# A two-layer graph network: one subtile in every two groups of tiles fetched row by row by SyncE

## The chip, the cores and the metric

The kernel runs on one core of a Trainium2 chip, in one launch. The metric is the device time of one execution in microseconds, the median of several runs. A core has TensorE (PE, matrix products), VectorE (DVE), ScalarE (ACT), GpSimd (POOL) and SyncE (SP); 16 DMA engines move data between device memory and the core's SBUF. Each engine runs its own stream of instructions and waits for the others through semaphores.

## The reference

A graph has 6250 nodes of 128 features and 200,000 edges, sorted by target (`dst`). Two layers run one after the other, each behind a layer norm and a ReLU and each added to `x`:

```
# layer 1: attention, 8 heads of 16
z  = h @ W;  el = z.attn_l;  er = z.attn_r
e  = leaky_relu(el[src] + er[dst], 0.2);  a = exp(e - max over dst)
out[dst] = sum(z[src] * a) / sum(a) + bias

# layer 2: an edge network (MUL = 32)
tpw = silu(silu(edge_attr_8 @ A1 + b1) @ A2 + b2) @ A3          # 4 x 32 weights per edge
messages from s[src], v[src] (s: 32, v: 32 x 3), edge_attr_4 and tpw
out[dst] = (sum of messages / 10) @ W_out
```

What matters here: in each layer, every edge needs one row of a node table, chosen by `src`. That is 200,000 random rows of 576 bytes (`z_tab`) and 200,000 of 512 bytes (`up_tab`).

## The kernel before

The edges are cut into 196 tiles (`NG`) of 1024 edges (`GE`), each of 8 subtiles (`T`) of 128 edges, one edge per partition. Four tiles (`U`) make a group; there are 49 groups (`GI`). The last tile has 3 subtiles (`LT`).

The program goes through these stages:

1. Set-up and the first node pass: norm and the product with `W`, whose rows are stored in `z_tab`.
2. Layer 1 over the groups. For every subtile POOL issues one indirect DMA (`gather`, L436) that brings 128 rows of `z_tab` into `rows[:, s, t, :]`, where `s` is the tile's slot (four slots) and `t` the subtile. DVE adds the target's score (L957, L958, L962), ACT takes the exponential (L555), DVE multiplies the rows by it (L966), and TensorE sums the products by target with a one-hot matrix (L1225), which DVE adds to the sums in SBUF (L883). In the middle of a group DVE finishes the node blocks that are complete by then (`finish_block`, L902 to L923) and SP stores them in `up_tab` (`store_up`, L372).
3. Layer 2 over the same groups, with rows of `up_tab`, two halves of four subtiles per tile (L1067 to L1079 for one half). SP loads the edge features two groups ahead (`load_ef` L390 and `load_y` L386, into two buffers each) and stores finished blocks of the output (L382).

What sets the order: each engine's stream is written out by hand. POOL, for group q and slot s, holds until TensorE has summed slot (s + 1) % 4 of the group before (slot 0 of the same group for s = 3), and then issues the 8 gathers of slot s. Each gather adds 16 to the semaphore `rows0` (subtiles 0 to 3) or `rows1` (4 to 7) of its slot, and DVE waits for `landed` on both. `msg1` of a slot counts the tiles that DVE has multiplied. `hold` is a wait that a register's value may enter, followed by a semaphore increment.

`groups` runs a body over 24 pairs of groups in a loop (`r`), with e = 0 and e = 1 written out in it, and once more for the 49th group. `blocks(eng, kind, at, work)` reads two words of the table `ready`, checks them and does `work` for the blocks between them, one per group on the mean. SP's part of layer 1 is before the change only a loop of 49 `store_up`; in layer 2 it is one `four_tiles` per group, that holds for `h1` (the edge network's first product of the group) ahead of `load_ef` and for `msg1` of slot 3 ahead of `load_y`. POOL waits for all stores of `up_tab` before layer 2.

Of the kernel before, what the change touches and what calls it, by code (L numbers as in the profile page):

```python
# [32 lines left out]
T = 8  # L33
# [8 lines left out]
PARTS = 64 + QUADS  # L42
ERP = 6 * HEADS
# [23 lines left out]
def gnn_kernel(nc, x, src, dst, dst_lin, edge_y, edge_f, bias, front, weights, out):  # L67

    with ExitStack() as ctx:
        def sb(name, shape, dt=F32):  # L70
            return ctx.enter_context(nc.sbuf_tensor(name, shape, dt))
# [66 lines left out]
        dst_rel = sb("dst_rel", [P, NG, T])  # L138
# [22 lines left out]
        rows = sb("rows", [P, U, T, ZW])  # L161
# [9 lines left out]
        def part(at, *shape, parts=P):  # L171
# [5 lines left out]
            if len(shape) == 1:  # L177
# [7 lines left out]
        tab_sb = rows[:, :, :, :].rearrange("p u t f -> p (u t) f")  # L185
# [52 lines left out]
                 ("x0", "x1", "front", "weights", "dst", "lin", "src", "bias", "win")}  # L238
# [6 lines left out]
            "sums_cleared", "ready_set", "cleared")}  # L245

        def named(tag, names):
            return {n: sem(f"{tag}_{n}") for n in names}
# [15 lines left out]
        s_l1 = named("edges", ("open", "er_sum")) | slot_sems("edges", ("spread", "square", "turned", "er", "scored", "score",  # L264
                                                         "exp", "msg0", "msg1", "agg", "added", "rows0", "rows1"))
        s_l2 = named("l2", ("h1", "h2", "tp", "first", "weighted", "dotted")) | slot_sems("l2", ("h1_act", "h2_act")) \
# [9 lines left out]
        def hold(eng, s, value):  # L276

            eng.wait_ge(s, value)
            eng.sem_inc(passed, 1)
# [10 lines left out]
        def last_blocks(eng, work):  # L290

            lo = eng.value_load(ready[0:1, GI + 1:GI + 2], min_val=0, max_val=NB - 1)
            with eng.Fori(lo, NB) as b:
                work(b)

        def groups(eng, body):

            with eng.Fori(0, GI // 2) as r:
                for e in range(2):
# [6 lines left out]
                   "rows1": [GI * 16 * HT] * (U - 1) + [(GI - 1) * 16 * HT]}  # L306
# [18 lines left out]
        def _(sp):  # L325
# [49 lines left out]

            sp.wait_ge(G["ready_set"], 1)
            with sp.Fori(0, NB) as b:
                store_up(b)
# [14 lines left out]
            with sp.Fori(0, passes1) as k:  # L393
                for buf in range(2):
                    load_ef(buf, buf)
                    load_y(buf, buf)

                def four_tiles(q, r, e):
                    n = sp.snap((passes1 + k) * GI + q + 1, min_val=1, max_val=2 * PASSES1 * GI)
                    m = sp.snap(k * (NG + AHEAD) + q * U, min_val=0, max_val=PASSES1 * (NG + AHEAD))  # L400
                    blocks(sp, mybir.EngineType.SP, q, store_block)
                    if isinstance(r, int):
                        return
# [6 lines left out]
                hold(sp, s_l2["h1"], (k + 1) * (NG + AHEAD))  # L410
                hold(sp, s_l1["added"][U - 1], (passes1 + k + 1) * QUADS)
# [14 lines left out]
        def _(pool):  # L426
# [7 lines left out]
            def gather(s, indices, table, width, done, n=T):  # L434
                for t in range(n):
                    pool.indirect_dma_start(out=rows[:, s, t, 0:width], out_offset=None, in_=table,  # L436
                                            in_offset=bass.IndirectOffsetOnAxis(ap=indices[:, t:t + 1], axis=0))\
                        .then_inc(done[t // HT], 16)
# [7 lines left out]
            with pool.If(general > 0):  # L446
                with pool.Fori(0, NG) as g:
                    hold(pool, s_max["idx"], g + 1)
                    gather(0, idx_max, z_tab, ZW, (s_max["rows"],) * 2)
# [164 lines left out]
        def _(dve):  # L614
# [234 lines left out]
            set_columns()  # L849
            own.after(v.tensor_copy(iota_l1, iota[:, :]))  # L850
# [76 lines left out]
            with dve.Fori(0, passes1) as k:  # L927
# [6 lines left out]
                def four_tiles(q, last):  # L934
# [3 lines left out]
                    landed = dve.snap(q * (16 * HT) + 16 * HT, min_val=16 * HT, max_val=GI * 16 * HT)  # L938
                    _, slots = nc.values_load_multi_w_load_instructions(
# [3 lines left out]
                    for s in range(U):  # L943
                        h = s % 2
                        ts = slice(0, LT if last and s == U - 1 else T)
                        el_e = rows[:, s, ts, MW:ZW]

                        if last and s == U - 1:
                            dve.wait_ge(s_l1["rows0"][s], ROWS_IN["rows0"][s])
                        else:  # L950
                            dve.wait_ge(s_l1["rows0"][s], landed)
                            dve.wait_ge(s_l1["rows1"][s], landed)
                        if s == 0:
                            dve.wait_ge(s_l1["added"][2], n)
                        else:
# [13 lines left out]
                            in1=rows[:, s, ts, 0:MW].rearrange("p t (h f) -> p t h f", f=RW),  # L969
# [59 lines left out]
            with dve.Fori(0, passes1) as k:  # L1029
# [8 lines left out]
                def four_tiles(q, r, e):  # L1038
# [4 lines left out]
                    landed = dve.snap(q * (16 * HT) + 16 * HT, min_val=16 * HT, max_val=GI * 16 * HT)  # L1043
                    _, low = nc.values_load_multi_w_load_instructions(
# [6 lines left out]
                    for s in range(U):  # L1051
                        h = s % 2
                        short = isinstance(r, int) and s == U - 1
                        for hf in range(1 if short else 2):
                            half = "rows0" if hf == 0 else "rows1"
                            dve.wait_ge(s_l1[half][s], ROWS_IN[half][s] if short else landed)
                            ts = slice(hf * HT, hf * HT + HT)
                            count = halves + (2 * s + hf + 1)
                            vecs = rows[:, s, ts, 0:96].rearrange("p t (i u) -> p t i u", u=MUL)
                            scal = rows[:, s, ts, 96:128]  # L1060
# [337 lines left out]
```

## Time and profile before

| | us |
|---|---|
| median of 3 runs | 4030.65 (4030.31 to 4036.2) |
| the profiled execution | 4040.77 |
| its span, first to last instruction | 4038.6 |
| mean granted TensorE clock | 0.806 of full speed |

The profile is of one execution. "Busy" is the time that an engine's instructions take; register work, branches and the issuing of DMAs are not counted in it. Layer 1 lies between about 95 and 2041 us of the span, layer 2 between about 2063 and 4028. The granted clock is 6 tenths in nearly all of layer 1 and 9 tenths in layer 2. In both, the slices of the page read 7 tenths busy for POOL, and the DMA engines are about 22% busy and move some 60 GB/s. A name with q behind it (SPq, DVEq, PEldq) is that engine's sequencer, which does register work and issues DMAs.

### The profile page before, as it was taken

The page shows a single profiled execution, that of the slowest core. Times are in us where ns is not written, and L with a number is a line of the kernel's source. Part 1 is how long each engine was busy: PE and PEld are TensorE (multiplying, and loading weights), DVE is VectorE, ACT ScalarE, POOL GpSimd, SP SyncE. Part 2 cuts the span into 40 slices and gives each one's busy share as a digit, 9 for nine tenths or more (in the row PEclk, how much of TensorE's full clock was granted, in tenths as well). Part 3 has the DMA queues.
Part 4 walks back from the last instruction along what each step waited for, and adds up shares of the span by engine and source line. Part 5 has one row for each costly group of instructions (what it writes and reads, how often), then busy time and mean ns, then how long its engine had stood idle before and what let it go on. Part 6 is the DMA issues. An engine that isn't in the chain of part 4 may idle for free.

```text
span 4038.6 us, 45135 instructions
## 1 busy us (share of the span) xinstructions
PE 2624.4 (65%) x11198; PEld 1908.9 (47%) x11199; DVE 2492.2 (62%) x6079; ACT 1012.0 (25%) x1447; POOL 2967.5 (73%) x3136
## 2 busy tenths in 40 slices
PE   3544454545555545445568888787888888888787
PEld 2444444444444444444445555555555555555554
DVE  7444444444444444444367777777877777777777
ACT  4333333333333333333231111111111111111111
POOL 2777777777777777777757777777777777777775
PEclk8666666666666666666679999999999999999999
DMA  4222222222222222222212222221222222222221
GB/s 126 61 60 61 60 61 60 60 60 60 60 60 60 60 60 61 60 60 61 60 49 59 59 59 60 58 60 57 60 58 59 59 59 59 59 60 59 59 59 48
DMA packets 139546, 245.74 MB, mean 61 GB/s; under 512 B 53965, under 2 KB 85815, under 8 KB 139415
## 3 DMA queue, kind: packets, MB, share of 16 engines
q0 software_dynamic: 100032, 217.87, 19.6%
q1 hardware_dynamic: 39352, 26.89, 2.3%
q10 hardware_dynamic: 144, 0.80, 0.1%
q14 instruction: 13, 0.10, 0.0%
q8 instruction: 5, 0.08, 0.0%
HBM read 235.32 MB, written 10.03 MB: 61 GB/s over the span
## 4 chain that ended last, share of the span: by engine, by line
POOL 54%; issue 23%; PE 9%; DVE 7%; DMA 4%; DVEq 1%; POOLq 0%; ACT 0%; ACTq 0%; SPq 0%
POOL rows L436 54%; PE pair L1225 5%; DMA rows<-z_tab,idx 3%; PE pair L1299 2%; DVE share L966 2%; DMA rows<-up_tab,idx 1%; DVE acc L869 1%; PE pair L1256 1%; PE pair L1139 0%; DVE share L957 0%; PE pair L1246 0%; DVE share L1074 0%; PE pair L1270 0%; PE pair L1250 0%; DVE share L1070 0%
## 5 line engine op out<-in xcount | busy, mean ns | idle before, releaser
L436 POOL DMA_INDIRECT rows<-z_tab,idx x1563 | 1488.3, 952 | 546.7 <-issue 525.3
L436 POOL DMA_INDIRECT rows<-up_tab,idx x1563 | 1477.7, 945 | 502.4 <-issue 486.6
L1225 PE MATMUL pair<-share,acc 128*128 128x136 f32 x3126 | 754.8, 433 | 842.2 <-DVE share L966 842.2
L1225 PEld LDWEIGHTS pair<-share,acc 128*128 128x128 f32 x3126 | 700.5, 326 | 975.9 <-DVE share L966 974.3
L1299 PE MATMUL pair<-share,acc 128*128 128x256 f32 x3126 | 808.7, 403 | 297.5 <-DVE share L1079 295.9
L1299 PEld LDWEIGHTS pair<-share,acc 128*128 128x128 f32 x3126 | 580.0, 195 | 677.8 <-DVE share L1079 576.3
L957 DVE TENSOR_TENSOR share<-rows,share 128x64 f32<-128x64 f32 x196 | 44.3, 226 | 899.9 <-DMA rows<-z_tab,idx 899.1
L1067 DVE TENSOR_TENSOR share<-rows,pair 128x384 f32<-128x384 f32 x391 | 216.6, 554 | 330.9 <-DMA rows<-up_tab,idx 320.4
L1256 PE MATMUL pair<-weights_sb,share 128*128 128x256 f32 x1576 | 397.0, 397 | 31.2 <-ACT acc L583 31.2
L570 ACT ACTIVATE share<-pair,front_sb 128x512 f32<-128x512 f32 x198 | 136.1, 687 | 1001.2 <-PE pair L1246 1001.2
L1256 PEld LDWEIGHTS pair<-weights_sb,share 128*128 128x128 f32 x1576 | 313.3, 201 | 87.4 <-issue 40.3
L555 ACT ACTIVATE pair<-share 128x64 f32<-128x64 f32 x196 | 44.6, 227 | 1119.3 <-DVE share L962 1119.3
L572 ACT ACTIVATE share<-pair,front_sb 128x512 f32<-128x512 f32 x198 | 136.1, 687 | 493.3 <-PE pair L1250 493.3
L966 DVE SCALAR_TENSOR_TENSOR share<-pair,rows 128x1088 f32<-128x1088 f32 x196 | 250.8, 1280 | 0.0
L869 DVE TENSOR_TENSOR acc<-acc,pair 128x1024 f32<-128x1024 f32 x197 | 240.4, 1220 | 0.1
L1005 DVE TENSOR_TENSOR acc<-acc,pair 128x1024 f32<-128x1024 f32 x197 | 238.9, 1213 | 0.0
L533 ACT ACTIVATE acc<-acc,ones 128x1024 bf16<-128x1024 bf16 x198 | 227.4, 1148 | 6.4
L1246 PE MATMUL pair<-ef_sb,weights_sb 64*128 64x512 f32 x396 | 225.7, 650 | 4.8 <-DMA ef_sb<-in_edge_f 4.1
L1074 DVE TENSOR_REDUCE share<-share 128x128 f32<-128x384 f32 x391 | 228.6, 585 | 0.0
L530 ACT ACTIVATE acc<-pair,acc 128x1024 bf16<-128x1024 f32 x198 | 218.2, 1102 | 20.4 <-PE pair L1172 20.4
L1070 DVE TENSOR_TENSOR share<-rows,pair 128x384 f32<-128x384 f32 x391 | 213.9, 547 | 0.0
L1076 DVE TENSOR_TENSOR share<-share,pair 128x384 f32<-128x384 f32 x391 | 212.3, 543 | 0.0
(167 smaller groups left out, 2384.4 us busy)
## 6 DMA issues: line engine op xcount, KB each, us to landing
rows<-z_tab,idx POOLq DMA_INDIRECT x1563, 2.5
rows<-up_tab,idx POOLq DMA_INDIRECT x1563, 2.5
ef_sb<-in_edge_f SPq DMA_DIRECT2D x50, 128.0 KB, 2.6
z_tab<-rows SPq DMA_DIRECT2D x7, 504.0 KB, 3.2
y_sb<-in_edge_y SPq DMA_DIRECT2D x50, 64.0 KB, 1.8
x_sb<-in_x SPq DMA_DIRECT2D x7, 448.0 KB, 7.0
up_tab<-acc SPq DMA_DIRECT2D x49, 64.0 KB
out<-x_sb SPq DMA_DIRECT2D x48, 64.0 KB
```

Source lines behind the costliest of these rows:

```text
L436: pool.indirect_dma_start(out=rows[:, s, t, 0:width], out_offset=None, in_=table, in_offset=bass.IndirectOffsetOnAxis(ap=indices[:, t:t + ...
L530: nc.scalar.activation(to, spread_ps, ACT.Square, bias=minus_id[:, bass.ds(tile, 1)])\
L533: nc.scalar.activation(to, to, ACT.Relu, bias=ones[:, 0:1], scale=-2.0).then_inc(s_l1["turned"][s], 1)
L869: v.tensor_tensor(hot[:, s, :, :], bc(dst_col[:, bass.ds(group, 1), :].rearrange("p a t -> p (a t)"), 2, P), bc(iota_l1, 1, T), ALU.is_equal)
L966: v.scalar_tensor_tensor(out=msg[:, h, ts, :].rearrange("p t (h f) -> p t h f", f=RW), in0=bc(a_ps[h][:, ts, :], 3, RW), scalar=1.0, in1=r ...
L1005: v.tensor_tensor(hot[:, s, :, :], bc(dst_col[:, bass.ds(group, 1), :].rearrange("p a t -> p (a t)"), 2, P), bc(iota_l2, 1, T), ALU.is_equal)
L1067: v.tensor_tensor(vy, vecs, y_v, ALU.mult)
L1074: v.tensor_reduce(dots, vy.rearrange("p t i u -> p t u i"), AX.X, ALU.add)\
L1225: mm = t.matmul(bank[2 + h][:, 0:MW], hot[:, s, i, :], msg[:, h, i, :], start=(i == 0), stop=(i == tiles - 1))
L1246: t.matmul(bank[4], a1_bd[at, s, :], ef_sb[at, :], start=True, stop=True).then_inc(s_l2["h1"], 1)
L1256: mm = t.matmul(bank[2 * (s % 2) + j // 2][:, (j % 2) * 256:(j % 2) * 256 + 256], h2_sb[:, s % 2, j * P:(j + 1) * P], a3_bd[:, :], start=T ...
L1299: mm = t.matmul(bank[6 + s % 2][:, 0:MSG], hot[:, s, j, :], msg2[:, s % 2, hf, j % HT, :], start=(j == 0), stop=(j == tiles - 1))
```

## The change

In every odd group (e = 1), the last subtile (t = 7) of slot 3 is no longer gathered by POOL. SP fetches its 128 rows one by one:

- `rows` becomes `rows_all` with 33 columns of 144 words instead of 32. The last one is `single`. In odd groups slot 3 uses columns 25 to 32 (`moved_on`) instead of 24 to 31: POOL fills the first seven of them and SP the eighth, so that DVE reads the eight side by side (`slot_rows`).
- The host lays out the 24 x 128 source indices of these subtiles as one row, `src_single` (12 KB). SP loads it into one partition, on top of `dst_rel`, which is free by then (`early`).
- `fetch_single` loads sixteen indices into SP's registers and issues sixteen DMAs of one row each, each adding 16 to the semaphore `single`. A pair of groups has 80 rows (`FIRST`) ahead of the blocks of its first group and 48 ahead of those of its second.
- There is one column, so SP holds for `msg1` of slot 3 of the odd group before the next pair's rows.
- SP's stores of layer 1 move into that loop. It waits for all rows of `z_tab` first, and for all stores of `up_tab` before layer 2.
- DVE waits for `single` as well. Its loop of layer 1 becomes one over pairs of groups.

```diff
+FIRST = 80
-        dst_rel = sb("dst_rel", [P, NG, T])
+        early = sb("early", [P, max(NG * T, GI // 2 * P)])
+        dst_rel = early[:, 0:NG * T].rearrange("p (g t) -> p g t", t=T)
+        single_i = early[0:1, 0:GI // 2 * P].bitcast(I32)
-        rows = sb("rows", [P, U, T, ZW])
+        rows_all = sb("rows", [P, U * T + 1, ZW])
+        rows = rows_all[:, 0:U * T, :].rearrange("p (u t) f -> p u t f", t=T)
+        moved_on = rows_all[:, (U - 1) * T + 1:U * T + 1, :]
+        single = rows_all[:, U * T, :]
...
+        FETCHED = 16 * P
+        def slot_rows(s, fetched):
+            return moved_on if fetched and s == U - 1 else rows[:, s, :, :]
+        def landed_beside(r, e):
+            return r * (32 * HT - 16) + (16 * HT + e * (16 * HT - 16))
...
@@ SP
+            def fetch_single(tab, width, r, first, last, fetched):
+                for c in range(first, last, 16):
+                    _, nodes = nc.values_load_multi_w_load_instructions(
+                        single_i[0:1, bass.ds(r * P + c, 16)], engines=(mybir.EngineType.SP,), min_val=0,
+                        max_val=NODES - 1, skip_runtime_bounds_check_because="they are sources, below NODES")
+                    for i, node in enumerate(nodes):
+                        sp.dma_start(single[c + i:c + i + 1, 0:width], tab[bass.ds(node, 1), 0:width])\
+                          .then_inc(fetched, 16)
+            sp.wait_ge(G["columns_set"], 1)
+            sp.dma_start(single_i, src_single).then_inc(loads["single"], 16)
+            sp.wait_ge(s_in["stored_early"], 16 * REUSED)
+            sp.wait_ge(s_in["stored"], 16 * (BI - REUSED))
+            sp.wait_ge(loads["single"], 16)
             sp.wait_ge(G["ready_set"], 1)
-            with sp.Fori(0, NB) as b:
-                store_up(b)
+            with sp.Fori(0, passes1) as k:
+                with sp.Fori(0, GI // 2) as r:
+                    for e, first, last in ((0, 0, FIRST), (1, FIRST, P)):
+                        fetch_single(z_tab, ZW, r, first, last, s_l1["single"])
+                        blocks(sp, mybir.EngineType.SP, r * 2 + (e + 1), store_up)
+                    hold(sp, s_l1["msg1"][U - 1], k * GI + r * 2 + 2)
+                hold(sp, s_l1["msg1"][U - 1], k * GI + GI)
+            last_blocks(sp, store_up, GI)
+            sp.wait_ge(s_mid["stored"], 16 * NB)
@@ SP, layer 2
-                    blocks(sp, mybir.EngineType.SP, q, store_block)
                     if isinstance(r, int):
+                        blocks(sp, mybir.EngineType.SP, q, store_block)
                         return
+                    fetch_single(up_tab, HIDDEN, r, *((FIRST, P) if e == 1 else (0, FIRST)), s_l2["single"])
+                    blocks(sp, mybir.EngineType.SP, q, store_block)
                     hold(sp, s_l2["h1"], m + U)
                     load_ef(e, q + 2)
                     hold(sp, s_l1["msg1"][U - 1], n)
                     load_y(e, q + 2)
@@ POOL
-                            gather(s, idx[:, e, s, :], tab, width, (s_l1["rows0"][s], s_l1["rows1"][s]),
-                                   LT if isinstance(r, int) and s == U - 1 else T)
+                            short, fetched = isinstance(r, int) and s == U - 1, e == 1 and s == U - 1
+                            gather(slot_rows(s, fetched), idx[:, e, s, :], tab, width,
+                                   (s_l1["rows0"][s], s_l1["rows1"][s]), LT if short else T - 1 if fetched else T)
@@ DVE, layer 1 (layer 2 likewise, for the second half of the tile)
                             dve.wait_ge(s_l1["rows0"][s], landed)
-                            dve.wait_ge(s_l1["rows1"][s], landed)
+                            dve.wait_ge(s_l1["rows1"][s], landed_3 if s == U - 1 else landed)
+                            if e == 1 and s == U - 1:
+                                dve.wait_ge(s_l1["single"], fetched)
-                with dve.Fori(0, GI - 1) as q:
-                    four_tiles(q, False)
-                four_tiles(GI - 1, True)
+                groups(dve, four_tiles)
```

## Rows read from the trace of the kernel before

**Rows 1.** Busy us (share of span) x instructions; then the chain that ended last, by engine.
```profile
PE 2624.4 (65%) x11198; PEld 1908.9 (47%) x11199; DVE 2492.2 (62%) x6079; ACT 1012.0 (25%) x1447; POOL 2967.5 (73%) x3136
...
POOL 54%; issue 23%; PE 9%; DVE 7%; DMA 4%; DVEq 1%; POOLq 0%; ACT 0%; ACTq 0%; SPq 0%
```

**Rows 2.** Groups by line, 200 to 2000 and 2200 to 4000 us: busy, mean | idle, releaser.
```profile
L436 POOL DMA_INDIRECT rows<-z_tab,idx x1437 | 1363.2, 949 | 438.0 <-issue 418.5 <-PE pair L1225 19.5
...
L436 POOL DMA_INDIRECT rows<-up_tab,idx x1441 | 1362.4, 945 | 439.3 <-issue 424.0 <-PE pair L1299 15.2
```

**Rows 3.** Waits, whole span: who waited for whom, us in total, times, longest.
```profile
DVE share L957 <- DMA rows<-z_tab,idx: 899.1, 146, 6.6
DVE share L1067 <- DMA rows<-up_tab,idx: 320.4, 186, 2.8
...
POOL rows L436 <- PE pair L1225: 21.0, 69, 0.3
...
SPq L372 <- DVE acc L923: 1920.4, 49, 79.7
```

**Rows 4.** Instructions of lines 372 and 386: duration ns min/median/max, first and last start.
```profile
L372 SPq ALU_OP  x49: 33/33/33, 151.0 to 2060.1; - x49
L372 SPq MOVE up_tab<-acc x49: 29/29/29, 151.1 to 2060.1; - x49
L372 SPq DMA_DIRECT2D up_tab<-acc x49: 338/339/366, 151.1 to 2060.2; - x49
...
L386 SPq DMA_DIRECT2D y_sb<-in_edge_y x50: 338/351/587, 2061.4 to 3987.6; - x50
```

**Rows 5.** SP's plain issues: line 342's durations; timeline (start, us) of issues without register work.
```profile
L342 SPq DMA_DIRECT2D win_dram<-share x4: 346/383/390, 15.5 to 16.8; - x4
...
15.53 1.63 SPq L342 DMA_DIRECT2D win_dram<-share  x4
...
2062.55 0.59 SPq L386 DMA_DIRECT2D y_sb<-in_edge_y  x1
```

**Rows 6.** Register loads, ns min/median/max: one word (L283), four (L939, L1187; its first two).
```profile
L283 DVEq TENSOR_LOAD <-ready x98: 309/318/329, 105.9 to 4017.3; - x98
...
L283 SPq TENSOR_LOAD <-ready x49: 268/279/296, 2063.4 to 3988.2; - x49
...
L939 DVEq TENSOR_LOAD <-slot_i x49: 341/352/379, 96.5 to 2006.1; - x49
...
L1187 PEldq TENSOR_LOAD <-slot_i x50: 547/1007/1022, 76.1 to 2009.6; - x50
```

**Rows 7.** Timeline between 2305 and 2323 us: DVE's last product of a group, SP's issues.
```profile
2306.76 0.28 DVE L1079 TENSOR_TENSOR share<-share,pair 128x128 f32<-128x128 f32 x1
...
2307.27 0.36 SPq L386 DMA_DIRECT2D y_sb<-in_edge_y  x1
...
2309.94 0.35 SPq L382 DMA_DIRECT2D out<-x_sb  x1
...
2322.18 0.52 SPq L390 DMA_DIRECT2D ef_sb<-in_edge_f  x1
```

**Rows 8.** DMA issues: queue, count, KB each, median us from issue to landing.
```profile
y_sb<-in_edge_y SPq DMA_DIRECT2D x50, 64.0 KB, 1.8
```

**Rows 9.** Timeline of DVE: the fourth tile of group 1, layer 1; one half tile, layer 2.
```profile
159.66 0.22 DVE L957 TENSOR_TENSOR share<-rows,share 128x64 f32<-128x64 f32 x1 [5.16 <-DMA rows<-z_tab,idx]
...
161.34 1.28 DVE L966 SCALAR_TENSOR_TENSOR share<-pair,rows 128x1088 f32<-128x1088 f32 x1
...
2430.04 0.55 DVE L1067 TENSOR_TENSOR share<-rows,pair 128x384 f32<-128x384 f32 x1
...
2432.33 0.28 DVE L1079 TENSOR_TENSOR share<-share,pair 128x128 f32<-128x128 f32 x1
```

**Rows 10.** Timeline at the layers' starts: first gathers, and the table that SP waits for.
```profile
72.45 1.18 POOL L436 DMA_INDIRECT rows<-z_tab,idx  x1 [70.53 <-issue]
...
94.92 0.17 DVE L862 CAST ready<-share 1x49 int32<-1x49 f32 x1
...
2063.22 0.94 POOL L436 DMA_INDIRECT rows<-up_tab,idx  x1 [26.30 <-issue]
```

**Rows 11.** The instruction queue: packets, MB, share of 16 engines.
```profile
q14 instruction: 13, 0.10, 0.0%
```

More of the change, by code:

```diff
@@ L64, in bc, with gnn_kernel @@
     return wide.broadcast_to(shape)
-def gnn_kernel(nc, x, src, dst, dst_lin, edge_y, edge_f, bias, front, weights, out):
+def gnn_kernel(nc, x, src, src_single, dst, dst_lin, edge_y, edge_f, bias, front, weights, out):
     with ExitStack() as ctx:
@@ L184, in gnn_kernel @@
         hT_sb = part(896, BU, P)
-        tab_sb = rows[:, :, :, :].rearrange("p u t f -> p (u t) f")
+        tab_sb = rows_all[:, 0:U * T, :]
         stats = part(2800, BU, 6)
@@ L237, in gnn_kernel @@
         loads = {n: sem(f"load_{n}") for n in
-                 ("x0", "x1", "front", "weights", "dst", "lin", "src", "bias", "win")}
+                 ("x0", "x1", "front", "weights", "dst", "lin", "src", "single", "bias", "win")}
         zeroed = sem("zeroed")
@@ L288, in blocks, with last_blocks @@
             return hi
-        def last_blocks(eng, work):
-            lo = eng.value_load(ready[0:1, GI + 1:GI + 2], min_val=0, max_val=NB - 1)
+        def last_blocks(eng, work, at=GI + 1):
+            lo = eng.value_load(ready[0:1, at:at + 1], min_val=0, max_val=NB - 1)
             with eng.Fori(lo, NB) as b:
@@ L410, in _ @@
                 hold(sp, s_l2["h1"], (k + 1) * (NG + AHEAD))
+                hold(sp, s_l1["msg1"][U - 1], (passes1 + k + 1) * GI)
                 hold(sp, s_l1["added"][U - 1], (passes1 + k + 1) * QUADS)
@@ L432, in _, with gather @@
             pool.memset(minus_id, 0.0).then_inc(zeroed, 1)
-            def gather(s, indices, table, width, done, n=T):
+            def gather(to, indices, table, width, done, n=T):
                 for t in range(n):
-                    pool.indirect_dma_start(out=rows[:, s, t, 0:width], out_offset=None, in_=table,
+                    pool.indirect_dma_start(out=to[:, t, 0:width], out_offset=None, in_=table,
                                             in_offset=bass.IndirectOffsetOnAxis(ap=indices[:, t:t + 1], axis=0))\
@@ L448, in _ @@
                     hold(pool, s_max["idx"], g + 1)
-                    gather(0, idx_max, z_tab, ZW, (s_max["rows"],) * 2)
+                    gather(rows[:, 0, :, :], idx_max, z_tab, ZW, (s_max["rows"],) * 2)
                 hold(pool, s_max["free"], NG + 1)
@@ L849, in _ @@
             set_columns()
+            dve.sem_inc(G["columns_set"], 1)
             own.after(v.tensor_copy(iota_l1, iota[:, :]))
@@ L933, in _, with four_tiles @@
                 v.memset(bank[3][:, 0:MW], 0.0)
-                def four_tiles(q, last):
+                def four_tiles(q, r, e):
+                    last = isinstance(r, int)
                     n = dve.snap(k * GI + q + 1, min_val=1, max_val=PASSES1 * GI)
@@ L938, in four_tiles @@
                     landed = dve.snap(q * (16 * HT) + 16 * HT, min_val=16 * HT, max_val=GI * 16 * HT)
+                    if not last:
+                        landed_3 = dve.snap(landed_beside(r, e), min_val=16, max_val=GI * 16 * HT)
+                        fetched = dve.snap((k * (GI // 2) + r + 1) * FETCHED, min_val=FETCHED, max_val=PASSES1 * GI * FETCHED)
                     _, slots = nc.values_load_multi_w_load_instructions(
@@ L945, in four_tiles @@
                         ts = slice(0, LT if last and s == U - 1 else T)
-                        el_e = rows[:, s, ts, MW:ZW]
+                        rows_s = slot_rows(s, e == 1)
+                        el_e = rows_s[:, ts, MW:ZW]
                         if last and s == U - 1:
@@ L1055, in four_tiles @@
                             half = "rows0" if hf == 0 else "rows1"
-                            dve.wait_ge(s_l1[half][s], ROWS_IN[half][s] if short else landed)
+                            dve.wait_ge(s_l1[half][s], ROWS_IN[half][s] if short else
+                                        landed_3 if s == U - 1 and hf == 1 else landed)
+                            if e == 1 and s == U - 1 and hf == 1:
+                                dve.wait_ge(s_l2["single"], fetched)
+                            rows_s = slot_rows(s, e == 1)
                             ts = slice(hf * HT, hf * HT + HT)
                             count = halves + (2 * s + hf + 1)
-                            vecs = rows[:, s, ts, 0:96].rearrange("p t (i u) -> p t i u", u=MUL)
-                            scal = rows[:, s, ts, 96:128]
+                            vecs = rows_s[:, ts, 0:96].rearrange("p t (i u) -> p t i u", u=MUL)
+                            scal = rows_s[:, ts, 96:128]
                             y_v = bc(y_ps[:, s, ts, 1:4], 3, MUL)
@@ L1345 @@
             .reshape(NG + U, P, T).transpose(1, 0, 2)),
+        "src_single": np.ascontiguousarray(
+            laid(src, 0, extra).reshape(GI, U, P, T)[1::2, U - 1, :, T - 1]).reshape(1, GI // 2 * P),
         "dst": np.ascontiguousarray(
```

17 lines of the change are left out of this document (10 added, 7 removed).

## The prediction

> **What bounds the kernel now.** I read the page's busy shares and its chain first [rows 1]: GpSimd (POOL) is busiest at 73%, and 54% of the chain that ended last is its gathers at L436, with 23% "issue", the time between them. Then the groups by line inside the two long stretches, one for each layer [rows 2]: 1437 gathers in 1800 us and 1441 in 1800 us, so one gather per 1.253 us and per 1.249 us, 0.95 us busy and 0.30 us of issue each. A gather fills one subtile (128 rows); a group of four tiles has 32 of them, a pair of groups 64, so a pair takes 80.2 us and 79.9 us: 80.05 in what follows. The list of waits says who follows whom [rows 3]: VectorE (DVE) waits for rows, 899.1 us in the attention layer (L957) and 320.4 us in the second (L1067), while POOL waits for TensorE 21.0 us at most. So POOL's gathers set the pace of both layers. DVE has 899.1/196 = 4.6 us of slack per tile in the first and 320.4/196 = 1.6 us in the second. SyncE (SP) has almost nothing to do now: it waits for DVE 1920.4 us at L372 alone.
>
> **What the change takes away.** In every odd group the fourth tile is gathered in 7 subtiles, not 8: 24 gathers fewer per layer, 48 in all. At 1.251 us each that is 60.0 us, all of it on the path, if nothing else becomes late: POOL's pair becomes 63 x 1.251 = 78.8 us.
>
> **What it adds.** SP fetches the missing subtile as 128 DMAs of one row, into one column. There is one such column, so SP may start on the next pair's rows only when DVE has multiplied the last ones (the hold on msg1 of the fourth tile). SP's turn is therefore a closed loop: hold, rows, landing, DVE's own work on that tile, and again. The pair takes whichever is longer, POOL's 78.8 us or this loop. Its terms:
>
> The row. Each has a register-based address on the DRAM side. At L372 the register work of such a DMA is ALU_OP 33 ns and MOVE 29 ns, and the issue itself 339 ns [rows 4]; four plain issues one behind another take 1.63 us at a median of 383 ns, so some 35 ns lie between instructions [rows 4, 5]. 0.339 + 0.033 + 0.029 + 3 x 0.035 = 0.51 us. Low end: the spacing of the plain issues, 0.42 us. High end: an issue behind another transfer took 0.59 us (L386, at 2062.55) [rows 5], with the same register work 0.75 us. I take 0.51, since one row is a small transfer and leaves little to queue behind: 128 x 0.51 = 65.3 us (53.8 to 96).
>
> The node numbers. Eight loads per pair, of sixteen words each. SP's load of one word takes 0.279 us. On DVE four words cost 0.352 against 0.318 for one: 0.011 us a word. On TensorE's sequencer two words cost 0.547 (the minimum, its first load) and four 1.007: 0.23 us a word [rows 6]. DVE reads from an index that is a multiple of four, TensorE from 4q + 3 (and from 1 in that first load). So a row of four that begins on a multiple of four seems to come in one step and any other word by word. SP's sixteen begin on a multiple of sixteen, so I count four steps: 0.279 + 15 x 0.011 + 3 x 0.23 = 1.13 us, with its address and gaps (0.12) 1.25, times eight 10.0 us. Low end, no extra steps: 0.57 x 8 = 4.6 us. High end, word by word: 0.279 + 15 x 0.23 + 0.12 = 3.85, times eight 30.8 us.
>
> The rest. DVE's L1079 ends at 2307.04 and SP's y_sb issue starts at 2307.27; 0.1 of that is the wake-up. From the end of that issue (2307.63) to the start of the out store (2309.94) lie a turn of the loop and one block's two loads, checks and branch: 2.31 us; with the store and its own branch 2.9 us [rows 7]. The second block of a pair lies behind the last row and is hidden by its landing. A y_sb transfer lands 1.8 us after its issue starts [rows 8], 1.45 us behind the issue; I take the same for a row (1.2 to 2.3). DVE then needs 159.66 to 162.62, 2.96 us, before the hold is released [rows 9]. Sum: 0.1 + 2.9 + 1.45 + 2.96 = 7.4 us. In the second layer DVE's part is the second half of the tile, 2430.04 to 2432.61, 2.57 us [rows 9], and SP also has two y_sb loads (0.5 and 0.6 us with their registers) and one ef_sb load (0.52 us, with hold and registers 0.8) [rows 7] before the last row: 7.0 + 1.9 = 8.9 us.
>
> SP's loop: 65.3 + 10.0 + 7.4 = 82.7 us in the first layer, 65.3 + 10.0 + 8.9 = 84.2 us in the second. Both are over POOL's 78.8 and over today's 80.05, by 2.65 and 4.15 us. The stall that goes (waiting for the 64th gather) is replaced by one for the rows of SP.
>
> **The ends.** In layer one POOL starts at 72.45 and is 23 us ahead when SP may begin, behind ready (94.92) [rows 10]; SP's first rows are used at 95.2 + 82.1 = 177.3 instead of 162.6: 14.7 us late. Behind the last turn POOL has run ahead by the buffers it has, two to three tiles, and the 49th group ends about 14 us sooner than at POOL's pace. So layer one costs 23 x 2.65 + 1 = 62 us. In layer two SP now waits for the last up_tab store before ef_sb (POOL did that already and starts at 2063.22); the start is late by some 2 us, the end gives 6 back, because DVE has less slack: 23 x 4.15 - 4 = 91 us. The doubled body of DVE's loop adds two register sums per group, hidden in its slack. The load of the single indices (12 KB) starts some 2 us ahead of ready and lands beside DVE's set-up. What the rows themselves move, 48 x 128 x 0.5 KB = 3.3 MB of 245.7, is nothing to DMA engines that are 22% busy.
>
> **Sum.** The profiled execution took 4040.8 us (span 4038.6): 4040.8 + 62 + 91 = 4194. The median of the runs is 10 us lower, 4030.65: 4184 us, 3.8% slower.
>
> **Two rules of the Trainium skill against the change.** Its page Runtime: NRT & Kernel Launch (Instruction fetch mechanics) says that a register load takes about 200 ns per register even in bulk. TensorE's rows agree (230 ns), DVE's (11 ns) do not. By that rule alone the 128 words cost 25.6 us in place of my 10.0, and the time would be near 4940. The same section says that an engine holds 512 instructions in blocks of 256 and that a branch back to a block no longer held stops it for a fetch. The instruction queue moved 13 packets in the whole run [rows 11], so no loop refetches today; SP's new body, 128 rows of three instructions and some 60 more, is about 450 long. By that rule each turn would have a stop more, which no row here prices; my sum has none, and 0 to 2 us a turn (0 to 96 us in all) stay in the range.
>
> **Rivals.**
> 1. SP keeps up, and all 60 us are gained: 3971 us. It takes a loop of 78.8 us or less: with my loads a row of 0.48 (layer one) and 0.466 us (layer two), or with loads of 4.6 us my row of 0.51, which gives 77.3 and 78.8. For it: DVE's slope of 11 ns a word, and plain issues spaced at 0.42 us. Against it: no addressed DMA of SP has less than ALU_OP, MOVE and 338 ns. This is the case that ends on the other side; it decides at a loop of about 80 us on the mean of both layers.
> 2. Break-even: a loop of 79.3 and 80.8 us, the saving of the first layer lost in the second: 4022 to 4039 us.
> 3. The words come one by one (the skill's rule, worked out from TensorE's rows): loads of 30.8 us, loops of 103.5 and 105.0 us, 24 x (23.45 + 24.95) = +1162 us, 5190 us. Against it: DVE's four in 0.352 us.
> 4. Issues queue behind each other's transfers at 0.59 us: a row of 0.75, loops of 113 and 115 us: about +1640 us. Against it: only issues behind a 128 KB load show it.
>
> **Chances.** Forecast (slower by the loop) 0.57; rival 1 0.29; rival 2 0.06; rival 3 0.05; rival 4 0.03. Faster by over 0.2% 0.29, within 0.2% (8 us, about what a measurement of this kernel can tell from none) 0.06, slower 0.65. The forecast's own range is 4060 to 4400: each 0.01 us of the row is 1.28 us a turn, 61 us in all, so a row of 0.49 to 0.54. The range of 8 in 10 takes in rival 1: 3968 to 4390.
>
> **What would show it.** Right: the spacing of SP's row issues near 0.51 us and of its 16-word loads near 1.25; DVE waiting at the fourth tile of odd groups for a DMA on SP's queue; POOL waiting for TensorE instead of 21 us some 3 to 5 us a pair; a pair of groups taking 83 and 84 us. Wrong: POOL's gathers still back to back at 1.25 us with SP idle at its hold, a pair of 78.8 us; or a load of sixteen words under 0.6 or over 3 us.

## The result and the profile after

The changed kernel takes 3973.39 us (3971.98 to 3976.1), the kernel before 4030.48 us on the same chip (4030.05 to 4036.2). The ratio is 0.9857, with a 95% interval of 0.9843 to 0.987: 57 us or 1.4% faster. The forecast was 4184 us, 3.8% slower. What happened is rival 1, "SP keeps up" (3971 us). Of all executions in this document one was slow, the fourth of experiment 6 (5162.53 us beside three of 3979), and its ratio leaves it out.

The page of the kernel after: busy us, share and count per engine; then the instruction queue; then the chain that ended last, by engine.

```profile
PE 2614.9 (66%) x11198; PEld 1907.8 (48%) x11199; DVE 2488.8 (63%) x6079; ACT 1012.2 (25%) x1447; POOL 2916.7 (73%) x3088
...
q14 instruction: 296, 2.42, 0.2%
...
POOL 45%; issue 21%; PE 13%; DVE 8%; DMA 8%; SPq 3%; DVEq 1%; ACT 1%; POOLq 0%; ACTq 0%
```

POOL has 48 instructions fewer than in [rows 1] and still leads the chain. Its gathers by line, first in the 1800 us from 200, then in the 1700 us from 2200:

```profile
L477 POOL DMA_INDIRECT rows<-z_tab,idx x1440 | 1362.2, 946 | 439.1 <-issue 412.9 <-PE pair L1280 26.2
...
L477 POOL DMA_INDIRECT rows<-up_tab,idx x1361 | 1285.6, 945 | 415.0 <-issue 383.0 <-PE pair L1354 32.0
```

That is one per 1.250 us and one per 1.249 us, the pace of [rows 2]. POOL is slowed in neither stretch, and a pair now has 63 gathers: 78.8 us. 48 x 1.25 = 60.0 us, of which 57.1 arrive.

The waits, whole span: who waited for whom, us in total, times, longest.

```profile
POOL rows L477 <- PE pair L1354: 35.1, 115, 0.3
...
DVE share L1007 <- DMA rows<-z_tab,idx: 854.2, 144, 6.6
DVE share L1122 <- DMA rows<-up_tab,idx: 273.1, 158, 2.3
...
DVE share L1007 <- DMA rows<-z_tab: 16.8, 2, 10.0
DVE share L1122 <- DMA rows<-up_tab: 12.7, 4, 3.8
...
SPq L285 <- DVE share L1016: 137.2, 24, 32.9
SPq L285 <- DVE share L1134: 42.6, 22, 9.5
```

The source without idx is SP's row by row fetch. DVE waited for it 6 times in all, and for POOL's gathers (with idx) 302 times. At L285, the hold, it is SP that waits: for 103.1 us in 22 waits between 200 and 2000 us (the first layer), for 41.8 us in 21 waits between 2100 and 3900 us (the second). So SP finishes each turn early, by little. Why its loop is shorter than I had worked out is in the rows of its two lines: durations in ns, min/median/max, then first and last start.

```profile
L399 SPq FUSED_REGOPS  x6144: 37/37/53, 97.3 to 3921.8; - x199
L399 SPq MOVE rows<-z_tab x3072: 29/29/38, 97.3 to 1966.7; - x192
L399 SPq DMA_DIRECT2D rows<-z_tab x3072: 230/237/325, 97.4 to 1966.8; - x192
...
L395 SPq TENSOR_LOAD <-early x384: 977/1144/1332, 96.0 to 3914.3; - x192
```

The issue of a row takes 0.237 us, not the 0.339 of [rows 4]. With its two register instructions and gaps the rows stand 0.42 us apart (from one start to the next, the median). A load of sixteen words takes 1.144 us; I had 1.13.

### The profile page after: what moved, and what is told of

Same layout as the page of the kernel before. It is cut to its first block, busy times and chain, and to the rows that moved or that the text cites. A ratio compares the mean times of both kernels' runs of the same rounds, so it can differ in the third digit from the quotient of the medians.

```text
span 3974.0 us, 64921 instructions
## 1 busy us (share of the span) xinstructions
PE 2614.9 (66%) x11198; PEld 1907.8 (48%) x11199; DVE 2488.8 (63%) x6079; ACT 1012.2 (25%) x1447; POOL 2916.7 (73%) x3088
## 4 chain that ended last, share of the span: by engine, by line
POOL 45%; issue 21%; PE 13%; DVE 8%; DMA 8%; SPq 3%; DVEq 1%; ACT 1%; POOLq 0%; ACTq 0%
POOL rows L477 45%; PE pair L1280 6%; DMA rows<-z_tab,idx 4%; PE pair L1354 4%; DMA rows<-up_tab,idx 3%; DVE share L1016 2%; SPq L399 2%; DVE acc L912 1%; DVE share L1129 1%; DVE share L1125 1%; PE pair L1311 1%; SPq L395 0%; DVE share L1123 0%; DVE share L1007 0%; DVE share L1134 0%
## 5 line engine op out<-in xcount | busy, mean ns | idle before, releaser
L477 POOL DMA_INDIRECT rows<-z_tab,idx x1539 | 1461.6, 950 | 539.7 <-issue 512.5
L477 POOL DMA_INDIRECT rows<-up_tab,idx x1539 | 1453.7, 945 | 495.5 <-issue 460.4
```

Source lines behind the costliest of these rows:

```text
L477: pool.indirect_dma_start(out=to[:, t, 0:width], out_offset=None, in_=table, in_offset=bass.IndirectOffsetOnAxis(ap=indices[:, t:t + 1], a ...
```

## The experiments

Ratios compare with the kernel before on the same chip, in the same set of runs. Its own time was 4030.51 us in the first set, 4038.07 in the second (the changed kernel would be at 4038.07 x 0.9857 = 3980 there), 4032.15 and 4029.57 beside the two probes.

**1. No rows on SP at all.** The column is zeroed once and SP fetches nothing; POOL keeps 63 gathers.

```diff
-                        fetch_single(z_tab, ZW, r, first, last, s_l1["single"])
...
-                    fetch_single(up_tab, HIDDEN, r, *((FIRST, P) if e == 1 else (0, FIRST)), s_l2["single"])
...
-                                dve.wait_ge(s_l1["single"], fetched)
...
-                                dve.wait_ge(s_l2["single"], fetched)
```

> The changed kernel without SyncE's row fetches (and without VectorE's wait for them): the eighth subtile of slot 3 in odd groups reads a column of zeros, so those edges are left out. POOL makes the same 63 gathers a pair. If POOL's gathers alone set the pace of the changed kernel (theory), nothing more is gained: 60 us below the kernel before, 3970 to 3973 us, the same as the changed kernel within 3 us. If SyncE's rows cost the changed kernel something (contention of 6144 small DMAs with the gathers, or a loop that is late in some turns), this one is faster than 3968.

Measured: 3972.02 us, 0.9855 (0.9838 to 0.9871). The 6144 row DMAs and 384 loads cost nothing that can be measured: 0.9855 against 0.9857. The limit is not on SP in either layer.

**2. One layer alone.** Layer 2 gathers all 64 subtiles as before; layer 1 is changed.

```diff
-            short, fetched = isinstance(r, int) and s == U - 1, e == 1 and s == U - 1
+            short, fetched = isinstance(r, int) and s == U - 1, tab is z_tab and e == 1 and s == U - 1
```

> The row fetches in layer 1 alone; layer 2 gathers all 32 subtiles as before the change. Theory (24 gathers of 1.251 us saved in each layer, both fully on the path): half of the gain, 4030.5 - 29 = 4001 us. If layer 2's SyncE loop already eats part of its saving, the remaining half is smaller and this kernel is nearer to the changed one: under 3995.

Measured: 4001.5 us, 0.9929 (0.9912 to 0.9946): 29.0 us of the 57. Each layer brings its half, 24 x 1.25 = 30.0 us less about one.

**3. A second gather less.** As in 1, and POOL also leaves out one subtile of the second tile: 62 gathers a pair.

```diff
-"rows1": [GI * 16 * HT] * (U - 1) + [(GI - 1) * 16 * HT - GI // 2 * 16]
+"rows1": [GI * 16 * HT, GI * 16 * HT - GI // 2 * 16, GI * 16 * HT, (GI - 1) * 16 * HT - GI // 2 * 16]
...
-            short, fetched = isinstance(r, int) and s == U - 1, e == 1 and s == U - 1
+            short, fetched = isinstance(r, int) and s == U - 1, e == 1 and s in (1, U - 1)
```

> As the run without rows, and the eighth subtile of slot 1 in odd groups is not gathered either (its column keeps old rows, so the result of those edges is wrong): 62 gathers a pair. Theory: POOL still sets the pace and another 48 x 1.251 = 60 us go: 3911 us. Rival: in layer 2 VectorE (79% busy) or TensorE (81%) takes over and only part of its 30 us comes: 3920 to 3941.

Measured: 3911.6 us, 0.9705 (0.9689 to 0.9721), 60.4 us under experiment 1. The second gather brings what the first did, so POOL sets the pace with room behind it on DVE and TensorE.

**4. The split of the rows over the pair.** 64 and 64 rows in place of 80 and 48.

```diff
-FIRST = 80
+FIRST = 64
```

> 64 rows ahead of the first block instead of 80 (FIRST = 64), the rest of the change as it is. Theory (a closed loop in which only the sum of the work counts, below POOL's 78.8 us): no difference, 3971 to 3976. Rival (the place of the blocks and of the edge-feature loads between the rows matters): over 3980 or under 3966.

Measured: 3974.05 us, 0.9859 (0.9843 to 0.9875). No difference: where in the turn the rows are issued does not matter while the turn as a whole is short enough.

**5. A small thing more per row.** One increment of a semaphore that nothing here waits for, behind each of the 128 rows. It asks how near SP is to its limit and what its loop contains.

```diff
                           .then_inc(fetched, 16)
+                        sp.sem_inc(passed, 1)
```

> One semaphore increment (0.08 us of SyncE's sequencer, nothing else) behind each row's DMA: 128 x 0.08 = 10.2 us more in each turn of SyncE's loop, which makes the row 0.50 us, what the prediction took it for. Theory (closed loop: the next rows wait for VectorE's use of the last ones; loops of about 75.5 us in layer 1 and 78.0 in layer 2 against POOL's 78.8): loops of 85.7 and 88.2, 23 x (6.9 + 9.4) = +375 us less some 15 at the layers' ends: 4325 to 4350 us. Rival (SyncE's throughput alone counts, landing and VectorE's part overlap the next rows: 72.4 and 75.6 us of work): +248 us, 4220 us. Rival (SyncE is far from the bound): 3973 us.

Measured: 4220.83 us, 1.0452 (1.0431 to 1.0473). By the total alone this is the number of the rival without a closed loop. The trace has to decide. The increment cost less than I had assumed: rows stand 0.494 us apart on average, where the changed kernel has 0.433 (both with the gaps inside the body): 0.061 more, 7.8 us a turn. The chain of waits of this run, then SP's loads between the first load of two turns that lie 18 turns apart, in layer 1 and in layer 2 (count, ns, first and last start), then the hold in the 1800 us from 200 and in the 1800 us from 2100:

```profile
SPq 60%; issue 31%; DVE 4%; DMA 2%; PE 1%; POOL 1%; DVEq 0%; ACT 0%; ACTq 0%; POOLq 0%
...
L395 SPq TENSOR_LOAD <-early x145: 981/1138/1242, 427.8 to 1922.7; - x145
...
L395 SPq TENSOR_LOAD <-early x145: 980/1143/1167, 2389.0 to 3921.3; - x145
...
SPq L285 <- DVE share L1017: 31.9, 21, 2.6
...
SPq L285 <- DVE share L1135: 4.7, 7, 2.8
```

145 loads are 18 turns of eight and one more. (1922.7 - 427.8)/18 = 83.05 us in layer 1, (3921.3 - 2389.0)/18 = 85.13 us in layer 2, where the changed kernel has 78.8 in both. SP now leads the chain with 60%. In layer 1 it still waits at its hold, 31.9/21 = 1.5 us a turn: that is the loop closed on itself. In layer 2 the waits come to 4.7 us in all. One turn's end in layer 1 shows the closed loop: SP's issues between 1325 and 1350 us and DVE's work between them (start, us).

```profile
1325.17 9.54 SPq L399 DMA_DIRECT2D rows<-z_tab  x17
1336.77 0.40 SPq L388 DMA_DIRECT2D up_tab<-acc  x1
1343.14 6.91 SPq L399 DMA_DIRECT2D rows<-z_tab  x14
...
1335.97 0.23 DVE L1008 TENSOR_TENSOR share<-rows,share 128x64 f32<-128x64 f32 x1 [19.81 <-DMA rows<-z_tab]
...
1337.65 1.28 DVE L1017 SCALAR_TENSOR_TENSOR share<-pair,rows 128x1088 f32<-128x1088 f32 x1
```

The last row's issue ends at 1325.17 + 9.54 = 1334.71; 1.26 us later it has landed and DVE starts, after 19.81 us of waiting; at 1338.93 DVE's product is done and the hold opens; at 1343.14 the next turn's first row is issued. SP's store at L388 lies inside that interval. A turn's end in layer 2 (SP's ef_sb load, the last instruction ahead of the hold that this view shows, and DVE's last product of the tile):

```profile
3064.77 0.52 SPq L429 DMA_DIRECT2D ef_sb<-in_edge_f  x1
...
3065.14 0.28 DVE L1135 TENSOR_TENSOR share<-share,pair 128x128 f32<-128x128 f32 x1
```

SP is done at 3065.29, DVE at 3065.42: SP comes to the hold when it is about to open. So the mechanism of the forecast exists in layer 1, where the closed loop adds some 1.5 us to SP's own 81.5. In layer 2 SP's own instructions fill the turn, and landing and DVE's part lie behind them, as the rival without a closed loop had it. In both layers SP's turn decides as soon as it is longer than 78.8 us. My expectation was 100 to 130 us too high, mainly because it took 0.08 us for the increment.

**6. A quarter of that.** The increment behind every fourth row.

```diff
+                        if i % 4 == 3:
+                            sp.sem_inc(passed, 1)
```

> The same increment behind every fourth row: 32 x 0.08 = 2.6 us more a turn. Theory: loops of 78.1 and 80.6 us: layer 1 still hidden behind POOL's 78.8, layer 2 over it by 1.8 us: 23 x 1.8 = +41 us, 4005 to 4015 us. Rival (throughput alone, 75.0 and 78.2): 3973 us.

Measured: 3978.99 us, 0.9853 (0.9834 to 0.9873), as the changed kernel; 4005 to 4015 us were expected. Its turns, and its hold in the 1800 us from 2100:

```profile
L395 SPq TENSOR_LOAD <-early x145: 974/1139/1187, 405.0 to 1820.1; - x145
...
L395 SPq TENSOR_LOAD <-early x145: 973/1145/1170, 2272.5 to 3695.9; - x145
...
SPq L285 <- DVE share L1136: 12.0, 9, 8.3
```

78.6 us in layer 1, and (3695.9 - 2272.5)/18 = 79.08 us in layer 2, with the waits at the hold all but gone (3.7 us in eight of them beside one of 8.3). The rows stand 0.443 us apart on average, 0.010 more than in the changed kernel. In layer 2 that has reached the edge. SP's turn is 0.3 us longer than POOL's 78.8, and it is 1.8 us over the 77.3 us that experiments 5 and 7 give below for the changed kernel: 0.06 us for each of 32 increments, not 0.08. DVE waits for SP's rows in 23 turns of that layer, 98.5 us in all. POOL keeps its pace even so, 1442 gathers in the 1800 us from 2100 where the changed kernel has 1441. 0.3 us a turn would be some 7 us in all, which is less than this measurement can tell, so a loss in time is not shown.

**7. The loads made slow.** The node numbers begin one word further on, so that no load starts on a multiple of four.

```diff
-        early = sb("early", [P, max(NG * T, GI // 2 * P)])
-        single_i = early[0:1, 0:GI // 2 * P].bitcast(I32)
+        early = sb("early", [P, max(NG * T, GI // 2 * P + 1)])
+        single_i = early[0:1, 1:GI // 2 * P + 1].bitcast(I32)
```

> The row of indices begins one word later in its partition, so that each load of sixteen words no longer begins on a multiple of four words; nothing else differs. Theory (a row of four aligned words comes in one step, any other word by word at 0.23 us): the load takes 0.28 + 15 x 0.23 = 3.7 us instead of 1.14, 8 x 2.6 = 20.8 us more a turn, loops of 96.3 and 98.8 us: 4800 to 4830 us. Rival (the address does not matter, sixteen words cost 1.14 us wherever they lie): 3973 us.

Measured: 4724.28 us, 1.1699 (1.1676 to 1.1723). The load, whole span, and 18 turns of each layer:

```profile
L395 SPq TENSOR_LOAD <-early x384: 3276/3438/3627, 96.3 to 4661.8; - x192
...
L395 SPq TENSOR_LOAD <-early x145: 3282/3441/3627, 469.7 to 2153.6; - x145
...
L395 SPq TENSOR_LOAD <-early x145: 3276/3438/3583, 2670.4 to 4392.5; - x145
```

A load takes 3.438 us, 2.294 more, 18.4 us a turn; I had 3.7 us, which is why the expectation was high. The turns are 93.55 and 95.67 us. This dose and that of experiment 5 give the changed kernel's own loop, which its trace can't show because SP waits: 93.55 - 18.4 = 75.2 and 83.05 - 7.8 = 75.3 us in layer 1, 95.67 - 18.4 = 77.3 and 85.13 - 7.8 = 77.3 us in layer 2. Two unlike doses agree within 0.1 us. SP's loop is 75.3 and 77.3 us, against POOL's 78.8: 3.5 and 1.5 us to spare.

**8. Half the rows.** SP fetches 64 of the 128 rows; the other 64 stay zero.

```diff
-        FETCHED = 16 * P
+        FETCHED = 16 * 64
...
-                    for e, first, last in ((0, 0, FIRST), (1, FIRST, P)):
+                    for e, first, last in ((0, 0, 48), (1, 48, 64)):
```

> SyncE fetches only the first 64 of the 128 rows (48 and 16; the other partitions of the column stay zero, so those edges are left out). Its loop body has some 230 instructions instead of 450. If the 2.6 us between the loop's branch and its next instruction are instruction blocks loaded anew in each turn, that gap falls below 0.5 us and the instruction queue's packets from 296 towards 13; if it is something of the branch itself, the gap stays. In time, theory: the loop is some 30 us shorter and nothing is gained, 3970 to 3973 us; if the changed kernel loses something to late rows, under 3970.

Measured: 3978.81 us, 0.9854 (0.9837 to 0.987): no gain from a shorter loop. Its trace shows something else, the fetch of instructions. Its instruction queue, then the end of a turn of layer 1 (DVE's product that opens the hold, SP's first row after it) and of layer 2 (SP's y_sb load behind the hold, its first row after that); below, the same of the changed kernel.

```profile
q14 instruction: 17, 0.14, 0.0%
...
1501.85 1.28 DVE L1017 SCALAR_TENSOR_TENSOR share<-pair,rows 128x1088 f32<-128x1088 f32 x1
...
1504.84 6.73 SPq L399 DMA_DIRECT2D rows<-z_tab  x16
...
2429.50 0.36 SPq L424 DMA_DIRECT2D y_sb<-in_edge_y  x1
2431.56 22.95 SPq L399 DMA_DIRECT2D rows<-up_tab  x48
```

```profile
1027.26 1.28 DVE L1016 SCALAR_TENSOR_TENSOR share<-pair,rows 128x1088 f32<-128x1088 f32 x1
...
1032.59 12.50 SPq L399 DMA_DIRECT2D rows<-z_tab  x26
...
2427.97 0.36 SPq L424 DMA_DIRECT2D y_sb<-in_edge_y  x1
2433.02 1.17 SPq L399 DMA_DIRECT2D rows<-up_tab  x3
```

From the end of DVE's product to the next row are 1504.84 - 1503.13 = 1.71 us with the short body and 1032.59 - 1028.54 = 4.05 us with the long one. In layer 2, from the end of the y_sb issue, they are 2431.56 - 2429.86 = 1.70 us and 2433.02 - 2428.33 = 4.69 us. The instruction queue moves 17 packets against 296 (13 before [rows 11], 344 with the increments of experiment 5, 155 with one layer of experiment 2, 14 without rows in experiment 1). So the turn of the loop costs 2.3 us more in layer 1 and 3.0 us more in layer 2 when the body, about 450 instructions long, has to be fetched again. The first of the two expectations came true: the stop at the branch went together with the packets. Four or five gaps of some 0.35 us inside the long body, where 0.03 to 0.06 are usual, are missing from the short one.

**9. What the issue is paid by.** Behind the last store SP issues plain DMAs of 1 to 128 rows of 512 B from x, four of each.

```diff
+            for n in (1, 2, 4, 8, 16, 32, 64, 128):
+                for i in range(4):
+                    sp.dma_start(probe[0:n, i, :], x[i * P:i * P + n, :]).then_inc(probed, 16)
+                done += 64
+                sp.wait_ge(probed, done)
```

> The changed kernel with measurements appended on SyncE behind the last store (its time is some 30 us longer by them): DMAs of 512 B rows of x to 1, 2, 4, 8, 16, 32, 64 and 128 partitions, four of each one behind another; then register loads of 1, 2, 4, 8 and 16 words from a row that begins on a multiple of sixteen words, and of 1, 2, 4 and 16 from one word later; and DMAs of one row with an address from a register. Theory A (the issue's time grows with the descriptors or the DMA engines that it feeds): 0.24 us for 1 partition, rising to 0.34 us for 16 and flat above (16 engines). Theory B (it grows with bytes or rows): 0.24 up to 8 or 16 partitions, and 0.34 only at 64 or 128. Loads: 0.28, 0.29, 0.32, 0.58 and 1.14 us aligned; one word later 0.28, 0.51, 0.97 and 3.7.

Measured (the issue of 1, 4, 16, 64 and 128 rows; ns min/median/max):

```profile
L469 SPq DMA_DIRECT2D rows<-in_x x4: 252/253/255, 3969.1 to 3970.0; - x4
...
L469 SPq DMA_DIRECT2D rows<-in_x x4: 261/296/297, 3973.6 to 3974.6; - x4
...
L469 SPq DMA_DIRECT2D rows<-in_x x4: 327/418/422, 3978.5 to 3979.8; - x4
...
L469 SPq DMA_DIRECT2D rows<-in_x x4: 587/594/597, 3984.4 to 3986.4; - x4
...
L469 SPq DMA_DIRECT2D rows<-in_x x4: 371/430/433, 3988.5 to 3989.9; - x4
```

Fewer rows are cheaper, but 64 cost more than 128, and here the bytes grow with the rows, so the cause was open; neither theory has these steps. Only the words of the loads of four were used, and only those loads are in the trace (0.49 and 0.56 us). Hence a second probe.

**10. Rows against bytes, and the loads by size.**

```diff
+            for n, w in ((1, 2), (1, 16), (1, P), (128, 2), (128, 16), (128, P), (1, P), (128, 2)):
+                for i in range(4):
+                    sp.dma_start(probe[0:n, i, 0:w], x[i * P:i * P + n, 0:w]).then_inc(probed, 16)
```

> The changed kernel with a probe at its end, behind the last store: SP issues plain DMAs from the input x, four of each shape one behind another, of 1 and of 128 partitions with 2, 16 and 128 words (8, 64 and 512 B) each; then it loads 1, 2, 4, 8 and 16 words of node numbers, from an index that is a multiple of 32 and from one behind it, and issues a row for each. Theory A (the issue is paid by the number of rows, that is of descriptors, that the DMA writes): 1 partition 0.24 to 0.26 us whatever its width, 128 partitions 0.34 to 0.43 us whatever their width. Theory B (by the bytes): 128 partitions of 2 words (1 KB) cost like one partition, 0.25 us, and 128 words in one partition more than 2 words in one. The loads, by the two sizes measured so far (sixteen aligned words 1.144 us, sixteen from one word further 3.44): in aligned fours, 0.28 for one word, 0.5 for four, 0.7 for eight, 1.14 for sixteen; off the multiple of four 0.21 us for each word more: 0.28, 0.49, 0.91, 1.75 and 3.44 us. If eight aligned words cost over 1.4 us, the step of four is wrong. The kernel's own time is the changed kernel's plus the probe, some 65 us more: 4035 to 4060.

Measured. First all twelve DMAs of one row (8, 64 and 512 B), then all twelve of 128 rows; then two loads each of 1, 2, 4, 8 and 16 words from a multiple of 32, and of 1, 2, 4, 8 and 16 words from one word further.

```profile
L469 SPq DMA_DIRECT2D rows<-in_x x12: 236/253/256, 3970.3 to 3975.3; - x12
L469 SPq DMA_DIRECT2D rows<-in_x x12: 341/432/433, 3976.6 to 3984.1; - x12
...
L474 SPq TENSOR_LOAD <-early x2: 451/453/455, 3991.4 to 3993.3; - x2
L474 SPq TENSOR_LOAD <-early x2: 643/644/644, 3995.2 to 3997.7; - x2
L474 SPq TENSOR_LOAD <-early x2: 474/475/476, 4000.3 to 4003.4; - x2
L474 SPq TENSOR_LOAD <-early x2: 690/695/700, 4006.6 to 4012.3; - x2
L474 SPq TENSOR_LOAD <-early x2: 1141/1142/1142, 4017.4 to 4026.4; - x2
...
L474 SPq TENSOR_LOAD <-early x2: 445/448/450, 4035.6 to 4037.4; - x2
L474 SPq TENSOR_LOAD <-early x2: 636/637/638, 4039.3 to 4041.8; - x2
L474 SPq TENSOR_LOAD <-early x2: 1035/1035/1035, 4044.3 to 4048.0; - x2
L474 SPq TENSOR_LOAD <-early x2: 1836/1836/1837, 4051.7 to 4057.9; - x2
L474 SPq TENSOR_LOAD <-early x2: 3439/3440/3440, 4064.1 to 4075.9; - x2
```

At both ends theory A holds and theory B does not: one row costs 0.253 us to issue whatever its width, 128 rows 0.432 us with 1 KB as with 64 KB. The shortest ones, 0.236 and 0.341 us, each the first of a four, are the 0.237 of the changed kernel's rows and the 0.339 of [rows 4]: the number of rows makes that difference by itself. Between the ends it is no straight line (64 rows, above). The loads go in aligned fours at 0.055 us a word, and off the multiple of four at 0.200 us a word; two aligned words (0.644) cost more than four (0.475). A load of one word takes 0.45 us here, each behind a wait, where [rows 6] have 0.279; the 0.28 that I had expected for it was wrong. The execution took 4089.58 us where I had expected 4060 at most: I had not counted the 124 rows that use the loads.

## Why the prediction was wrong

**What bounds the kernel** held: POOL's gathers before and after, 1.25 us each (experiments 1 to 3).

**What the change takes away**, 60.0 us, held: 58.5 us come when SP does nothing, 57.1 with its rows. Some 1.5 us of the 60 are missing without any rows too; where they go was not looked into. The rest, 1.4 us, is within what can be measured.

**The row is the step that failed.** I argued "0.339 + 0.033 + 0.029 + 3 x 0.035 = 0.51 us". The 0.339 is the issue of a transfer over 128 rows; no DMA on SP in the trace before had fewer than 50. That the issue depends on the shape could be seen even there: ef_sb's load, of 64 rows, took 0.52 us, y_sb's, of 128, took 0.36 [rows 7]. A DMA of one row is issued in 0.237 us (experiments 9 and 10 show that the number of rows is the reason), and the spacing is 0.42 us, 0.433 with the gaps inside the body. 128 x 0.433 = 55.4 us, not 65.3: 9.9 us a turn. I wrote that one row is "a small transfer and leaves little to queue behind" and used it only to choose 0.51 between the ends, without asking whether the issue itself depends on the shape. The low end of 0.42, from the spacing of plain issues, was right by luck: those had no register work and dearer issues (0.346 to 0.390 us).

**The node numbers** held: 1.144 us for my 1.13, and the reading behind it (fours that begin on a multiple of four in one step, other words one by one) is what experiments 7 and 10 show. The Trainium skill's page Runtime: NRT & Kernel Launch (Instruction fetch mechanics) says that a register load takes about 200 ns per register even in bulk; that page speaks of registers filled from device memory, and here the words lie in SBUF. Off the multiple of four that is exact, 0.200 us; on it, sixteen words cost 0.69 us more than one.

**The rest** held in its parts and lacked one. Landing was 1.26 us behind the issue for my 1.45, and DVE's part 1338.93 - 1335.97 = 2.96 us as forecast. But in layer 1 the loop of 75.3 us less 55.4 for the rows and some 9.9 for the loads (8 x 1.144 and 0.1 each for address and gaps) leaves 10.0 us, where I had 7.4; in layer 2 12.0 us, where I had 8.9. The instruction fetch that I had left out of the sum accounts for nearly all of it, 2.3 of 2.6 us in layer 1 and 3.0 of 3.1 us in layer 2 (experiment 8). The same section of the Trainium skill says that a branch back to a block no longer held stops the engine for a fetch; the instruction queue's 296 packets and the 4.05 and 4.69 us at the turn agree. My bound for it, 0 to 2 us a turn, was about half of what came: beside the 2.3 and 3.0 us there are the four or five gaps inside the body, which the 0.433 us of a row contains. In layer 2 the sum also had the parts in the wrong roles: I counted landing and DVE's part, hid SP's last block behind them and left out its second ef_sb load. Both take about equally long (in the turn of experiment 5 shown above, 3.57 us for landing and DVE and 3.44 us for SP's own work, from the end of the last row's issue at 3061.85), so the sum hardly changes by it.

**The closed loop** is real in layer 1 and hardly there in layer 2, and in neither is SP's turn the limit. The 75.3 and 77.3 us are both below 78.8, where I had 82.7 and 84.2. Experiments 5 and 7 make SP's turn the limit. Experiment 5 has 4.3 and 6.3 us a turn over POOL's pace, 24 x 10.6 = 254 us by that, and 241 were measured (4220.83 - 3980). The margin is thin: with the row at 0.443 us, experiment 6, layer 2 is on the edge.

**The rivals.** Rival 1 named its own condition, a row of 0.48 and 0.466 us (by its sum 0.468); the row was 0.433. What I held against it ("no addressed DMA of SP has less than ALU_OP, MOVE and 338 ns") was true of the rows and proved nothing, as all of those were transfers of 64 rows or more. Rivals 3 and 4 needed 3.85 us a load and 0.75 us a row; neither came. **The marks of the wrong case** were as written: gathers back to back at 1.25 us, SP idle at its hold, a pair of 78.8 us.

**Chances.** 0.29 for rival 1 was too low. It needed a row only 0.03 to 0.042 us shorter than the one I took, out of bounds that reached 0.09 below, and the one duration under the sum came from another shape of transfer. The range held the time, by 5 us at its low end.

## What to carry to other kernels

When a queue is to issue many small DMAs, price the issue by a DMA with as few rows; where the trace has none, the price of a wide one was the upper end here and no middle. The turn of a helping queue (issue, land, use, release, or its own instructions if they take longer) costs nothing until its length passes the period of the engine that bounds the kernel, and then costs in full, so compare the two lengths first: here 75.3 and 77.3 against 78.8 us. One further gather a pair taken from GpSimd is worth 30 us a layer here (experiment 3), but SP has no room left for it: ScalarE, busy 25% of the span, was not tried.

## What was not expected of the hardware

- SP issues a DMA of one row in 0.253 us (0.237 with an address from a register) and one of 128 rows in 0.432 us, the same for 8 and 512 B a row. 64 rows of 512 B took 0.594 us, more than 128; why was not looked into.
- A register load of 16 words takes 1.142 us from a multiple of 32, and 3.440 us from one word further. That one word made the kernel 19% slower (experiment 7 against the changed kernel's ratio: 1.1699/0.9857).
- A loop of some 450 instructions on SP's queue is fetched again in each turn: 296 packets instead of 13, and 2.3 us at the branch in layer 1, 3.0 us in layer 2. With a body of half the rows there were 17 packets and no such stop.
- One semaphore increment per row, 17 ns long, made the rows 0.061 us further apart, and 128 of them a turn the kernel 6% slower (1.0452/0.9857).
